# Sixteen heads of an output product in three units of a tile: 8, 3 and 5 in place of 6, 4 and 6

## The reference, cut to what matters

```python
def _L0_xattn_ref(image_embeds, latents, ln1_g, ln1_b, ln2_g, ln2_b, Wq, Wkv, Wo):
    x = layer_norm(image_embeds, ln1_g, ln1_b)
    l = layer_norm(latents, ln2_g, ln2_b)
    q = l @ Wq
    kv_in = jnp.concatenate([x, l], axis=1)
    k, v = jnp.split(kv_in @ Wkv, 2, axis=-1)
    q, k, v = (to_heads(q), to_heads(k), to_heads(v))
    w = jnp.einsum('bhqd,bhkd->bhqk', q * scale, k * scale)
    w = jax.nn.softmax(w.astype(jnp.float32), axis=-1).astype(q.dtype)
    out = jnp.einsum('bhqk,bhkd->bhqd', w, v)
    out = out.transpose(0, 2, 1, 3).reshape(B, S_lat, INNER)
    return out @ Wo
x = _layernorm(x + _L0_attn_ref(x, ...))
x = _layernorm(x + _L0_xattn_ref(ctx_1024, x, ...))
x = _layernorm(x + _L0_ffn_ref(x, ...))
```

## Time and profile before

| | |
|---|---|
| median of 3 runs | 1544.98 us (1544.03 to 1548.81) |
| the profiled execution | 1550.83 us |
| its span | 1548.9 us |
| TensorE matmuls busy | 1376.8 us, 89% |
| ScalarE busy | 1149.7 us, 74% |
| VectorE busy | 1135.8 us, 73% |
| GpSimd busy | 902.6 us, 58% |
| mean granted TensorE clock | 0.961 |

### The profile page before, as it was taken

One profiled execution on the slowest core, in us unless ns is written; L12 is line 12 of the kernel. 1 busy time (PEld: TensorE's weight loads), 2 busy tenths in 40 slices (PEclk: granted clock), 3 DMA queues, 4 the chain that ended last, 5 costly groups with the idle time before them and its releaser, 6 DMA issues. The chain is left out here.

```text
span 1548.9 us, 37505 instructions
## 1 busy us (share of the span) xinstructions
PE 1376.8 (89%) x10765; PEld 1290.8 (83%) x10765; DVE 1135.8 (73%) x4170; ACT 1149.7 (74%) x4085; POOL 902.6 (58%) x1233
## 2 busy tenths in 40 slices
PE   6799999999999999999999999999994799999940
PEld 4699899898998899989999899998983798898830
DVE  4467777777777777777777777777665687787765
ACT  3588888888888888888888888888872455555535
POOL 4455666666666666666666666666544255555565
PEclk8899999999999999999999999999997799999975
DMA  3000000000000000000000000000003776777746
GB/s 91 11 11 11 17 15 17 19 15 17 15 17 19 15 17 15 17 19 15 17 15 17 19 15 17 15 17 8 10 10 59 219 238 210 220 227 219 218 148 192
DMA packets 64629, 96.24 MB, mean 62 GB/s; under 512 B 10892, under 2 KB 48786, under 8 KB 64306
## 3 DMA queue, kind: packets, MB, share of 16 engines
q1 hardware_dynamic: 44738, 71.90, 15.7%
q0 software_dynamic: 8896, 16.94, 3.2%
q10 hardware_dynamic: 10800, 5.06, 1.2%
HBM read 71.55 MB, written 23.35 MB: 61 GB/s over the span
## 5 line engine op out<-in xcount | busy, mean ns | idle before, releaser
L698 ACT ACTIVATE probs<-ps_s,neg_max 128x128 f32<-128x128 f32 x1024 | 361.7, 365 | 163.7 <-DVE neg_max L945 160.6
L513 POOL TENSOR_TENSOR probs_n<-probs,inv_sum 128x512 f32<-128x512 f32 x256 | 266.8, 1042 | 219.2 <-DVE inv_sum L951 211.7
L1367 PE MATMUL ps_s<-kvT,u_sb 128*128 128x128 f32 x2048 | 274.8, 277 | 0.8 <-issue 0.8
L1380 PE MATMUL ps_o<-value_w,tT 128*128 128x128 f32 x2048 | 260.2, 275 | 1.9 <-ACT tT L716 1.8
L1367 PEld LDWEIGHTS ps_s<-kvT,u_sb 128*128 128x128 f32 x2048 | 254.4, 191 | 7.0 <-issue 1.0
L1380 PEld LDWEIGHTS ps_o<-value_w,tT 128*128 128x128 f32 x2048 | 244.1, 192 | 2.9 <-ACT tT L716 2.9
L956 DVE TENSOR_TENSOR pT_lo<-ps_pT,pT_hi 128x512 fp32r<-128x512 f32 x256 | 175.5, 686 | 84.9 <-ACT pT_hi L707 84.9
L611 POOL DMA_INDIRECT y_rows<-wvT,f_id x144 | 145.1, 1008 | 154.7 <-DVE wvT L1284 100.2
L945 DVE TENSOR_REDUCE neg_max<-ps_s 128x4 f32<-128x512 f32 x256 | 176.9, 691 | 42.7 <-PE ps_s L1367 32.2
L698 ACT ACTIVATION_READ_ACCUMULATOR probs<-ps_s,neg_max 128x1 f32 x1024 | 207.4, 203 | 0.0
L1390 PE MATMUL ps_pT<-ident,probs_n 128*128 128x128 f32 x1024 | 157.7, 276 | 37.5 <-DVE pT_lo L956 36.6
(11 more groups left out here) (274 smaller groups left out, 3564.7 us busy)
## 6 DMA issues: line engine op xcount, KB each, us to landing
u_sb<-in_expert_w SPq DMA_DIRECT2D x45, 578.0 KB
tT<-in_expert_w SPq DMA_DIRECT2D x27, 578.0 KB
f_x<-x_rows SPq DMA_DIRECT2D x72, 130.0 KB
tT<-y_rows SPq DMA_DIRECT2D x16, 512.0 KB, 4.7
x_raw<-in_x SPq DMA_DIRECT2D x64, 64.0 KB, 1.8
c_raw<-in_ctx_in SPq DMA_DIRECT2D x64, 64.0 KB, 2.0
out<-u_sb ACTq DMA_DIRECT2D x16, 256.0 KB, 2.3
y_rows<-wvT,f_id POOLq DMA_INDIRECT x144
```

What stands on the lines that cost most here:

```text
L513: nc.gpsimd.tensor_tensor(probs_n[:, sl], probs[:, sl], inv_sum[:, sl, :].rearrange("p (u o) -> p u o", o=1).to_broadcast([P, UP, P]), ALU ...
L698: last = nc.scalar.activation(probs[:, sl, j], ps_s[sl][:, j * P:(j + 1) * P], ACT.Exp, bias=neg_max[:, sl, j:j + 1], accum_out=sums[:, sl ...
L1367: last = nc.tensor.matmul(ps_s[sl][:, j * P:(j + 1) * P], u_sb[:, c // 2, BT * p + b, h:h + 2].rearrange("p h s -> p (h s)"), kvT[:, c, 2 ...
L1380: last = nc.tensor.matmul(ps_o[:, 0:D], tT[:, (p + 1) % 2, h], value_w[:, h], start=(h == 0), stop=(h == H - 1))
```

## The change

`out_part` makes heads 0 to 7 in unit 1, 8 to 10 in unit 2 and 11 to 15 in unit 3. It made 0 to 5, 6 to 9 and 10 to 15. The waits of each unit stay where they were.

```diff
@@ -1375,7 +1375,7 @@
                     pe.wait_ge(z2_done, t - 1)
                 if k == 2:
                     pe.wait_ge(t_done, 4 * t)
-                lo, hi = ((0, 6), (6, 10), (10, 16))[k - 1]
+                lo, hi = ((0, 8), (8, 11), (11, 16))[k - 1]
                 for h in range(lo, hi):
                     last = nc.tensor.matmul(ps_o[:, 0:D], tT[:, (p + 1) % 2, h], value_w[:, h],
                                             start=(h == 0), stop=(h == H - 1))
```

## The result

| | before | after |
|---|---|---|
| median | 1546.61 us (4 runs, 1544.03 to 1548.81) | 1524.51 us (4 runs, 1522.81 to 1528.25) |
| ratio | | 0.9864, 95% interval 0.9834 to 0.9895 |
| profiled span | 1548.9 us | 1523.4 us |
| a plain tile of the loop | 17.50 us | 17.09 us |

The forecast was 1521.4 us, 23.6 us less than the 1544.98 us of the three runs known then; the medians differ by 22.1 us, the spans by 25.5. With a fourth run the median before is 1546.61 us, which accounts for 1.6 of the 3.1 us between the forecast and the time measured. The first row is the page's group for L1390 (busy us, mean ns, then idle us before it and its releaser), the second the busy time of each engine from 600 to 700 us.

A forecast was written before the change was run, and what follows sets the result against it. A ring of TensorE work and a VectorE, ScalarE and GpSimd chain bounds the tile; 0.22 + 0.19 = 0.41 us a tile, 56 x 0.41 + 0.6 = 23.6 us off 1544.98 gives 1521.4 us, range 1516 to 1535.

The forecast's parts named there:

- a ring: Steady tile: TensorE 5.90 and 4.66 us, 1.18 to unit 0's maxima, 5.77 from these to unit 1's turning; sum 17.51.
- Unit 1, two heads more, at no cost: Ahead of the turning of the probabilities (L1390): 0.45 us more TensorE work, hidden in a wait of 0.73 us.
- Unit 2, 0.22 us: One head fewer on TensorE between unit 1's turning and unit 3's scores: 0.22 us off the 5.90.
- Unit 3, 0.19 us in place of 0.22, because of VectorE's queue: One head fewer between unit 3's and unit 0's scores; VectorE's L899 ahead of unit 0's maxima leaves 0.19 of 0.22 us.
- L1447: TensorE in unit 3, overwriting the bank ScalarE's L690 copies out: matmul 0.03 us late, no more than VectorE's limit takes.
- L875 beside GpSimd's L507: VectorE after unit 3's maxima: nothing counted for starting 0.22 us sooner; if held, 0.38 us a tile gained, 1523 us.
- How often: 0.41 us a tile in tiles 4 to 58, 55 times, and once more in the tile behind them.
- The end of the loop: Last five tiles: one more gain of 0.41 us, two with estimated gains of 0.3 us each, two without a wait.
- Behind the loop: Expert stage after the loop: not touched, starting that much earlier.
- The slower rival: VectorE's copies L1031, L1033 run into GpSimd's L513 in every tile: 0.55 - 0.41 = 0.14 us more, 1553 us; chance 0.06.

The follow-up runs named there:

- The chain shortened by 0.63 us without a change of heads: VectorE's L1021 moved behind L976, heads 6, 4, 6, against the kernel before: 16.86 us a tile, median 1514.33 us, ratio 0.9797.
- the run with 8, 4, 4: Heads split 8, 4, 4 in place of 6, 4, 6, against the kernel before: 17.32 us a tile, median 1538.37 us, ratio 0.9952.
- the run with the late copies: L906 put ahead of L1027, L1031, L1033 in the kernel after (8, 3, 5): 17.18 us a tile, median 1531.29 us, ratio to before 0.9866.
- the routing away from L513: L1027, L1031, L1033, L1021 moved behind L976 in the kernel after: 16.77 us a tile, ratio to before 0.9691; with 6, 4, 6, 16.75 us, 0.9698.

## Why the prediction was right, point by point

- *What bounds the kernel*: a ring of TensorE from unit 1's turning to unit 3's scores, and VectorE's and ScalarE's chain back to the turning. Right. The chain shortened by 0.63 us without a change of heads took 0.64 us off the tile.
- *Unit 1, two heads more, at no cost*: right. They cost 0.45 us of TensorE's time inside the wait, and 0.32 us of the wait is left. The forecast's numbers give 0.73 - 0.45 + 0.03 = 0.31, the last term because VectorE's chain came forward by 0.19 only where TensorE came forward by 0.22.
- *Unit 2, 0.22 us*: right. From the turning in unit 1 to the scores of unit 3 it was 5.90 us, and 0.22 of it went. With both heads out of this unit it is 0.44.
- *Unit 3, 0.19 us in place of 0.22, because of VectorE's queue*: right, and the run with 8, 4, 4 shows the limit by itself. The one number read from a cadence (an instruction starts 0.09 us before the end of the one ahead, so 0.38 us between the starts of L899 and the maxima) was off by 0.01 or 0.02: they are 0.39 to 0.40 us apart when nothing is waited for. I overlooked what fills this queue. VectorE's L1014, 128x8 like L1021, stands ahead of L899, and it too is held by an L513, for 0.96 us, in each of the 54 tiles and in every kernel of this study. It and L513 after:

```profile
589.14 1.04 POOL L513 TENSOR_TENSOR probs_n<-probs,inv_sum 128x512 f32<-128x512 f32 x1 [1.55 <-DVE inv_sum L951]
...
589.25 0.96 DVE L1014 TENSOR_TENSOR mask<-picked 128x8 bf16<-128x8 f32 x1
```

  No run moved L1014, so what unit 3's heads are worth without that hold is open.
- *L1447*: right. The load waits, and the matmul is late by 0.01 us; the forecast allowed 0.03.
- *L875 beside GpSimd's L507*: it started 0.23 us sooner against L507 and took 0.35 us for the pair (0.34 before). The timeline of all engines after:

```profile
586.88 0.72 POOL L507 TENSOR_TENSOR rs_qk<-se_qk,m_half 128x2 f32<-128x2 f32 x1
...
587.30 0.35 DVE L875 TENSOR_TENSOR turned<-qkv,sinb 128x64 f32<-128x64 f32 x2
```

  The Trainium skill, SBUF — State Buffer, section Who interferes with whom, would have it blocked until 587.60. The measurement decides: a GpSimd instruction of two elements a row does not hold it for its 0.72 us, while L513, of 512 elements a row, holds L1033 and L1021 to its end. Whether L507 holds the ports for a part of its time isn't settled by these rows.
- *How often*: right for tiles 4 to 58. L1427 of tile 58 starts 22.3 us sooner, and since it now has 0.45 us more work ahead of it in its own tile, the loop is 22.8 us ahead there; the forecast was 55 x 0.41 = 22.6.
- *The end of the loop*: wrong by 1.3 us. I had put 1.0 us of gain on the last tiles; at the last matmul of the routing, L1571, the kernel after is 22.5 us ahead (1188.1 and 1165.6), so they gave back 0.3. In these tiles the profile names VectorE's L982, L976 and L1014, ScalarE's L716 and GpSimd's L513 for TensorE's waits; I hadn't followed them one by one, and the 0.3 us each had no row behind it.
- *Behind the loop* nothing was to change. The span shows 3.0 us more (22.5 at L1571, 25.5 at the end), of which 2.3 come before the last norm (1501.6 and 1476.8 for its first L818). It isn't in the medians, whose difference is 22.1, and the runs of the kernel before alone lie 4.8 us apart. From L1571 to the end it is 360.8 us before and 357.7 after, and 354.9 to 363.0 in the profiled executions of all nine kernels, which have the same expert stage. So 3 us are within its spread; where that comes from no run shows. That the forecast of 23.6 lies near the spans' 25.5 is in part luck: the 1.3 us too many at the end of the loop and these 3.0 go opposite ways.
- *The slower rival*: its mechanism is real, and it didn't come about. The four longer tiles are there after too, at 17.54 to 17.64 us. The offset between VectorE's copies and GpSimd's scaling stayed, as forecast, since ScalarE still waits ahead of the exponentials. Its price of 0.55 us wasn't tested: the run with the late copies costs 0.09 us a tile, but it has L906 ahead of the copies, as the rival hasn't. The traces show where the 0.55 come from. In a plain tile L906 starts ahead of L513 (605.08 and 605.20), L1021 is held, and L911, which reads what L906 writes, starts as the hold ends, 0.98 us after L513 (606.18). In a longer tile L1033 is held first, and L906 stands behind it. A tile like that after, VectorE and L513 from the timeline of all engines:

```profile
370.67 0.23 DVE L1027 TENSOR_SCALAR routed<-gexp,den_i 128x2 f32<-128x2 f32 x1 [0.26 <-issue]
...
370.81 0.29 DVE L1031 COPY routed<-rows 128x256 f32<-128x256 f32 x1
...
370.85 1.14 POOL L513 TENSOR_TENSOR probs_n<-probs,inv_sum 128x512 f32<-128x512 f32 x1
...
371.01 1.00 DVE L1033 COPY routed<-rids 128x2 int32<-128x2 int32 x1
...
371.93 0.34 DVE L906 SCALAR_TENSOR_TENSOR z<-ps_a,rs_qk,x_raw 128x128 f32<-128x128 f32 x1
...
372.37 0.29 DVE L911 BATCH_NORM_STATS2 st_z<-z 128x6 f32<-128x128 f32 x1
```

  L911 starts 1.52 us after L513 here, 0.54 more, which is the whole lengthening. It is L906 that starts as the hold ends, and L911 follows 0.44 us later; the other 0.10 is L513, which takes 1.14 us in place of 1.03.

  VectorE stood 0.26 us here without waiting for anything that the profile shows. This comes once in nine tiles in each kernel whatever the tile's length, so it goes with the place in the program and not with time. What it is stays open. With the routing away from L513 it does next to no harm: no longer tile was left with 8, 3, 5, and with 6, 4, 6 three tiles take 16.81 to 16.84 us.

## What to carry to other kernels

Write the steady loop as a ring of starts, with each step given to one engine: work taken out of a step gains only if the step is in the ring, and only until the next limit, so the same head was worth 0.22, 0.19 or 0 us depending on the unit it left. Before filling a wait with other work, look at what is late at its end: here one VectorE instruction of 0.15 us that took 0.92 was worth more than the whole rearrangement, and once it and the copies beside it were moved the rearrangement was worth nothing. The best kernel of this study has 8, 3, 5 and the routing behind L976, at 0.9691 of the time before; 6, 4, 6 with the same edit is as good.

## What the runs showed of the hardware

VectorE instructions of two or eight elements a row took 0.91 to 1.01 us in place of 0.15 or 0.16 when GpSimd's L513 (128x512, 1.04 us) had started shortly ahead of them, and it was whichever of L1033 and L1021 came first that paid. Behind L976, away from L513, both took 0.15 or 0.16. The hold also goes the other way by a little: in the longer tile shown above, where L1031 was in flight as L513 started, L513 took 1.14 us. I had expected such a hold for rare tiles only, and had not seen that the plain tile pays it each time, 0.63 us in the chain that sets the time, and once more on L1014.
